# Destination bases of a sort read from a table instead of carried from step to step, and its record loads issued by SyncE

## The chip, the cores and the metric

The kernel runs on one core of a Trainium2 chip. The metric is the device time of one launch in microseconds (us); less is better. PE is the matrix engine, DVE the vector engine, ACT the scalar engine, POOL the GpSimd engine, SP the sync engine.

## The reference

Four graph layers on 6250 nodes with 128 features and 100000 edges, each added to its input:

```python
edge_index = jnp.stack([src, dst])          # src unsorted, dst sorted
for each of four layers:                    # attention, gated message, update, filter
    h = jnp.maximum(_layernorm(x), 0.0)
    x = x + layer(h, src, dst, edge attributes)   # gathers by one index, segment sums by the other
```

The first layer's attention needs for each edge a term of its destination, its softmax runs over the edges with one source (`segment_max` and `segment_sum` by `src`), and its sums run by `dst`. The later layers sum by either index. For this the kernel orders the edges by source before the layers run.

## The kernel before, in words

The edges are padded to 100352 = 784 tiles of 128 edges (`T`), the nodes are 49 blocks of 128 (`NB`). Eight tiles (`GT`) make a step, so a stage over all edges has 98 steps. The key of an edge is split into the number within its block (low part) and the block (high part).

The stages that the change touches run one after the other, with a barrier between them:

- `constants` makes the identity, triangular and all-ones matrices and loads keys and nodes.
- `front`, 98 steps: DVE makes one-hot rows of the low and high parts (L408, L409). PE sums them: `hs` counts the edges of each source (L466), and `hd` adds up over all steps, through an all-ones matrix, how many edges of each destination block stand in tile 0, 1, ... 7 of a step (L468). DVE reduces `hd` over the eight tiles to the 49 totals `tot_dst` (L416). The attention terms of the nodes are made beside it.
- `offsets`: from the counts, prefix sums give each source's first place (`start`) and each destination block's first place (`excl`, copied to `base_dst`, L585). 56 matmuls (L531) count slots meanwhile.
- `sort`, 98 steps: for each edge its place in the order by source (`rank`, into `idx`), its place in the order by destination (`drank`, kept in the record at `W_POS`) and its destination's attention term (`sj`, into the record at `W_SJ`) are worked out. POOL then writes each tile's 128 records of 512 bytes to `src_records` at those places, with one indirect DMA per tile (`send`, L798), 784 in all.

How `sort` is ordered: each engine runs its own loop, written by `run_steps` from a list of (stage, lag): in round r the stage works on step r - lag. The rounds of the engines are tied by semaphores alone:

- SP: `load_rows` (lag 0) loads the keys' low parts, spread over all partitions (two DMAs, L612), into one of two buffers.
- ACT: `load_records` (0), `wide_hot` (1), `low` (0), `keys` (2), `mask` (1), `carry` (2).
- PE: `prefix` (1), `same` (1), `late` (3), `rank` (2), `drank` (2), `early` (2).
- DVE: `bump` (2), `place` (3), `hot` (0), `finish` (3). The end of `finish` counts `placed` up (L676).
- POOL: `send` (0), which waits for `placed` and `keyed`.

The records lie in four buffers. `load_records` of step s waits until all eight sends of step s - 4 have landed (`sent`), and is the first thing in ACT's round. The destination bases are a running row: `drank` of a step starts from `dbase` (L759), adds the edges before it in its tile (L762) and the tiles before it (eight matmuls, L766), whose last 49 columns are the row for the next step. ACT copies them back to `dbase` in `carry` (L708), and `place` of step s doesn't take `drank` before that copy is done:

```python
wait_step(e, r["dranked"], st)
e.wait_ge(r["carried"], st.i + 2)
e.tensor_tensor(r["pick"][:, 0, :, :], ...)          # L657
```

Of the kernel before, what the change touches and what calls it, by code (L numbers as in the profile page):

```python
# [5 lines left out]
ALU = mybir.AluOpType  # L6
ACT = mybir.ActivationFunctionType
F32 = mybir.dt.float32
# [5 lines left out]
P = 128  # L14
# [4 lines left out]
GT = 8  # L19
# [198 lines left out]
def setup(kn, ctx):  # L218
# [22 lines left out]
    kn.base_dst = sb("base_dst", [P, NB])  # L241
# [10 lines left out]
    kn.tot_dst = sb("tot_dst", [P, NB])  # L252
# [19 lines left out]
def constants(kn):  # L272

    def sb(name, shape, dt):
# [5 lines left out]
        sb(n, [P, P], F16) for n in ("beforeh", "penh", "identh", "onesh", "iotah"))  # L280
    kn.kin = sb("kin", [P, 2, T], I32)
# [5 lines left out]
    def build(r):  # L287
# [7 lines left out]
        def vector(e, ch):  # L295
# [15 lines left out]
            ch(e.tensor_copy(kn.identh[:, :], kn.ident[:, :]))  # L311
            ch(e.tensor_copy(kn.onesh[:, :], kn.ones[:, :]))
# [46 lines left out]
def front(kn):  # L359
# [6 lines left out]
    def build(r):  # L366
        def vector(e, ch):
            e.memset(r["zero"][:, :], 0.0).then_inc(r["zero_ok"], 1)

# [46 lines left out]
            ch(e.tensor_reduce(kn.tot_dst[:, :], r["hd"][:, 0:GT * NB].rearrange("p (t b) -> p b t", b=NB), AX, ALU.add))  # L416
# [17 lines left out]
        def tensor(e, ch):  # L434
            for i in range(total):
# [27 lines left out]
                if i < n:  # L463
# [4 lines left out]
                    e.matmul(r["hd"][:, 0:GT * NB], kn.onesh[:, :], r["hi"][:, i % 2, 0, :, :].rearrange("p t b -> p (t b)"),  # L468
# [30 lines left out]
        def sync(e, ch):  # L499
            e.wait_ge(r["zero_ok"], 1)  # L500
            for c in range(7):
# [9 lines left out]
                 ("sij", [P, NB * 2 * HEADS], F32)],  # L511
# [4 lines left out]
def offsets(kn):  # L516
# [5 lines left out]
    def build(r):  # L522
        def tensor(e, ch):
            e.matmul(r["small"][:, 0:NB], kn.before[:, :], kn.count[:, 1, :], start=True, stop=True)
            e.matmul(r["small"][:, NB:2 * NB], kn.ones[:, :], kn.count[:, 1, :], start=True, stop=True,
                     skip_group_check=True).then_inc(r["sums"], 1)
# [11 lines left out]
        def vector(e, ch):  # L538
            ch(e.tensor_scalar(r["none"][:, :], kn.count[:, 1, :], 0.0, None, ALU.is_equal))
# [5 lines left out]
            ch(e.tensor_copy(r["tot"][:, 0:NB], kn.tot_dst[:, :]))  # L545
# [28 lines left out]
            for q in range(2):  # L574
                for c in range(nt):
                    ins = e.tensor_scalar(r["lt"][:, q, c, :], r["s"][:, :], r["val"][:, q, c:c + 1], None, ALU.is_gt)
                ins.then_inc(r["less"], 1)
            e.wait_ge(r["counted"], 2)
# [6 lines left out]
            ch(e.tensor_copy(kn.base_dst[:, :], r["excl"][:, 0:NB]))  # L585
            ch.wait()
            for q in range(2):
# [9 lines left out]
                      ("none", [P, NB], F32)],  # L597
               sems=["sums", "iota", "less", "counted"])


def sort(kn):
# [5 lines left out]
    def build(r):  # L607
        def sync(e, ch):
# [6 lines left out]

            e.wait_ge(kn.low_st, 32)
            run_steps(e, ch, [(load_rows, 0)], n)

        def vector(e, ch):
            e.memset(r["rec"][:, :, :, :], 0.0).then_inc(r["cleared"], 1)  # L620
            ch(e.memset(r["onerow"][:, :], 1.0))
# [27 lines left out]
            def place(st):  # L649
# [6 lines left out]
                e.wait_ge(r["carried"], st.i + 2)  # L656
# [22 lines left out]
        def scalar(e, ch):  # L679
            def load_records(st):  # L680
                wait_quad_free(e, r, "sent", st, GT)
                e.dma_start(r["rec"][:, st.quad, :, 0:NREC], rec_tiles[:, bass.ds(st.i * GT, GT), :]
                            ).then_inc(r[f"rec_ld{st.quad}"], 16)

# [21 lines left out]
            def carry(st):  # L706
                wait_step(e, r["dranked"], st)
                e.activation(r["dbase"][0:1, :], r["drank"][0:1, GT * NB:], ACT.Copy).then_inc(r["carried"], 1)  # L708

# [4 lines left out]
            e.wait_ge(r["cleared"], 1)  # L714
            e.activation(r["dbase"][0:1, :], kn.base_dst[0:1, :], ACT.Copy).then_inc(r["carried"], 1)
            run_steps(e, ch, [(load_records, 0), (wide_hot, 1), (low, 0), (keys, 2), (mask, 1), (carry, 2)], n, 4)
            ch.wait()

        def tensor(e, ch):
# [1696 lines left out]
```

## Time and profile before

| | |
|---|---|
| Median of three runs | 7450.98 us (7444.45 to 7451.76) |
| Profiled execution, own time | 7452.6 us |
| Its span, first to last instruction | 7451.0 us |
| Busy over the span | PE 65%, PE weight load 50%, DVE 63%, ACT 35%, POOL 60% |
| First to last send of `sort` | 332.4 to 1583.9 us |
| Mean granted clock of TensorE | 0.719 |

A span is read from the first instruction to the last; the own time of the profiled execution is 1.6 us longer. A line such as "ACT x L698 <- DMA y: 485.3, 50" says that ACT sat idle before its instruction of line 698 for 485.3 us in 50 cases, and that a DMA which writes y ended each of these. A share of busy time is a mean over some twenty stages with different limits; the change lies in the stages that end at 1596 us.

### The profile page before, as it was taken

Reading aid. Unit: us, or ns where it says so; the run is one execution under the profiler, and the core shown is the slowest. Engines: PE = TensorE matmul, PEld = TensorE weight load, DVE = VectorE, ACT = ScalarE, POOL = GpSimd, SP = SyncE. Lnnn points to the kernel's source line nnn. Section 1 sums busy time; section 2 is a strip of 40 time slices with the busy share of each in tenths; the row PEclk is TensorE's granted clock in tenths of the full one; section 3 lists DMA queues with packets and bytes.
Section 4 is the critical chain, followed back from the end, with each engine's and each line's share of the span. In section 5 each row is a group of like instructions: output and inputs, shape, how many; then the busy total and the mean of one; then the engine's idle time right before and its main releaser. Section 6 shows DMA issues by size and latency. Waiting matters only on the chain. (4 is left out here: it accounts for less than half of the span.)

```text
span 7451.0 us, 136629 instructions
## 1 busy us (share of the span) xinstructions
PE 4824.4 (65%) x26170; PEld 3695.7 (50%) x26171; DVE 4677.1 (63%) x15439; ACT 2640.5 (35%) x6893; POOL 4448.7 (60%) x5261
## 2 busy tenths in 40 slices
PE   6777777730555554773566666666667664998896
PEld 4555555520444443662355555334555554666664
DVE  8666665634444443666555555777777775777776
ACT  2244444410222222664400000563333334444443
POOL 0165666652777777662277777207777771777774
PEclk9978787765555555666566667788888886778777
DMA  1144444460222222441133333103333321333332
GB/s 59 51 119 118 120 119 119 117 71 20 58 58 58 58 57 71 113 112 48 43 78 78 78 78 78 25 15 78 74 74 74 75 68 31 73 72 72 72 72 52
DMA packets 858580, 541.08 MB, mean 73 GB/s; under 512 B 652181, under 2 KB 757481, under 8 KB 858089
## 3 DMA queue, kind: packets, MB, share of 16 engines
q0 software_dynamic: 148032, 300.00, 14.9%
q1 hardware_dynamic: 608520, 192.51, 12.5%
q10 hardware_dynamic: 101920, 47.37, 2.6%
q8 instruction: 40, 0.66, 0.0%
q14 instruction: 68, 0.55, 0.0%
HBM read 411.68 MB, written 127.68 MB: 72 GB/s over the span
## 5 line engine op out<-in xcount | busy, mean ns | idle before, releaser
L1339 POOL DMA_INDIRECT l2e_rows<-l_rows,l2e_idx x832 | 847.2, 1018 | 566.9 <-DVE l2e_idx L1347 328.4
L798 POOL DMA_INDIRECT src_records<-sort_rec,sort_idx x784 | 768.5, 980 | 552.4 <-DVEq L676 319.4
L1339 POOL DMA_INDIRECT l1e_rows<-l_rows,l1e_idx x832 | 796.8, 958 | 490.0 <-DVE l1e_idx L1347 296.3
L1339 POOL DMA_INDIRECT l3e_rows<-l_rows,l3e_idx x832 | 804.1, 967 | 424.8 <-DVE l3e_idx L1347 221.4
L1222 POOL DMA_INDIRECT dst_rows<-l0d_out,l0d_idx x832 | 812.3, 976 | 276.5 <-issue 196.7
L2115 PE MATMUL l2e_pV<-l2e_rows,ident 128*128 128x512 f32 x416 | 302.3, 817 | 355.6 <-DMA l2e_rows<-l_rows,l2e_idx 355.1
L1194 PE MATMUL l0d_pX<-table,l0d_ohT 128*128 x1664 | 461.2, 457 | 86.3 <-issue 69.3
L1321 PE MATMUL l0m_pR<-l0m_rows,l0m_oh 128*128 128x129 f32 x1664 | 352.8, 378 | 200.2 <-DVE h_nodes L1292 140.9
L1685 PE MATMUL l1e_pG<-k_weights,l1e_dT 64*128 64x128 f32 x1664 | 220.5, 403 | 374.7 <-DVE l1e_prod L1714 371.7
L1194 PEld LDWEIGHTS l0d_pX<-table,l0d_ohT 128*128 128x128 f32 x1664 | 393.1, 326 | 139.8 <-issue 139.7
L1186 PE MATMUL l0d_pT<-identb,l0d_oh 128*128 128x128 bf16 x832 | 125.4, 305 | 472.8 <-DVE l0d_oh L1167 472.8
L1321 PEld LDWEIGHTS l0m_pR<-l0m_rows,l0m_oh 128*128 128x128 f32 x1664 | 306.4, 276 | 246.7 <-issue 199.9
L1714 DVE TENSOR_TENSOR l1e_prod<-l1e_pG,l1e_rows 128x512 f32<-128x512 f32 x208 | 143.9, 692 | 447.9 <-DMA l1e_rows<-l_rows,l1e_idx 425.3
L1705 ACT ACTIVATE l1e_dT<-l1e_pD 128x256 f32<-128x256 f32 x208 | 79.9, 384 | 970.4 <-PE l1e_pD L1674 970.4
L2139 ACT ACTIVATE l2e_sq<-l2e_pV 128x128 f32<-128x128 f32 x832 | 219.1, 278 | 554.9 <-PE l2e_pV L2120 554.9
L1695 PE MATMUL l1e_pR<-l1e_oh,l1e_prod 128*128 128x128 f32 x1664 | 387.1, 405 | 6.3 <-DVE l1e_prod L1714 4.6
L1685 PEld LDWEIGHTS l1e_pG<-k_weights,l1e_dT 64*128 64x128 f32 x1664 | 169.6, 274 | 443.7 <-ACT l1e_dT L1705 174.7
L1130 DVE TENSOR_TENSOR l0d_t<-l0d_meta,l0d_dump 128x4 f32<-128x4 f32 x208 | 35.7, 172 | 555.9 <-DMA dst_rows<-l0d_out,l0d_idx 555.9
L2245 PE MATMUL l3e_pR<-l3e_oh,l3e_prod 128*128 128x128 f32 x1664 | 307.8, 342 | 103.9 <-issue 53.7
L2120 PEld LDWEIGHTS l2e_pV<-table,l2e_ohT 128*128 128x128 f32 x1664 | 296.5, 251 | 142.8 <-issue 142.8
L1695 PEld LDWEIGHTS l1e_pR<-l1e_oh,l1e_prod 128*128 128x128 f32 x1664 | 330.7, 295 | 47.2 <-issue 40.5
L2245 PEld LDWEIGHTS l3e_pR<-l3e_oh,l3e_prod 128*128 128x128 f32 x1664 | 259.9, 238 | 188.9 <-issue 188.3
(406 smaller groups left out, 13955.7 us busy)
## 6 DMA issues: line engine op xcount, KB each, us to landing
sort_rows<-lo_rows SPq DMA_DIRECT2D x196, 256.0 KB
sort_rec<-rec ACTq DMA_DIRECT2D x98, 472.0 KB
l0m_rows<-dst_rows SPq DMA_DIRECT2D x416, 66.0 KB, 2.0
l0m_rows<-dst_rows POOLq DMA_DIRECT2D x416, 66.0 KB
l1e_rec<-src_records SPq DMA_DIRECT2D x832, 32.0 KB
l2e_lrow<-dst_local SPq DMA_DIRECT2D x208, 128.0 KB
l3e_rec<-src_records SPq DMA_DIRECT2D x832, 25.0 KB
l0d_meta<-src_records SPq DMA_DIRECT2D x832, 6.0 KB
```

Source lines behind the costliest of these rows:

```text
L798: e.indirect_dma_start(kn.by_src_rec[:, :], bass.IndirectOffsetOnAxis(ap=r["idx"][:, st.quad, j:j + 1], axis=0), r["rec"][:, st.quad, j, : ...
L1194: ins = e.matmul(r["pX"][:, st.par, j, 0:TW], r["ohT"][:, st.quad, j, :], kn.tab0[:, bass.ds(blocks[j] * TW, TW)], start=True, stop=True)
L1222: e.indirect_dma_start(kn.by_dst[:, :], bass.IndirectOffsetOnAxis(ap=r["idx"][:, st.quad, j:j + 1], axis=0), r["out"][:, st.quad, j, :], N ...
L1321: ins = e.matmul(sums(r, st, j), r["oh"][:, st.par, j, :], r["rows"][:, st.ring, j, 0:AW], start=True, stop=True)
L1339: e.indirect_dma_start(r["rows"][:, st.quad, j, 0:width], None, table[:, :], bass.IndirectOffsetOnAxis(ap=r["idx"][:, st.quad, j:j + 1], a ...
L1685: ins = e.matmul(r["pG"][:, st.par, q, u * P:(u + 1) * P], r["dT"][at, st.par, u, :], w[at, :], start=True, stop=True)
L1695: ins = e.matmul(r["pR"][:, st.par, j, :], r["prod"][:, st.par, j, :], r["oh"][:, st.par, j, :], start=True, stop=True)
L1714: e.tensor_tensor(r["prod"][:, st.par, :, :].rearrange("p (u q) c -> p q u c", q=2), r["pG"][:, st.par, :, 0:2 * P].rearrange("p q (u c) - ...
L2115: e.matmul(r["pV"][:, st.quad, :, :].rearrange("p j c -> p (j c)"), kn.ident[:, :], r["rows"][:, st.quad, :, :].rearrange("p j c -> p (j c ...
L2120: ins = e.matmul(r["pV"][:, st.quad, j, :], r["ohT"][:, st.par, j, :], block(kn, kn.TB, blocks[j]), start=False, stop=(j == G - 1), skip_g ...
L2139: ch(e.activation(r["sq"][:, j, :], r["pV"][:, st.quad, j, :], ACT.Square, scale=H ** -0.5, accum_out=r["var"][:, st.par, j:j + 1]))
L2245: ins = e.matmul(r["pR"][:, st.par, j, :], r["prod"][:, st.par, j, :], r["oh"][:, st.par, j, :], start=True, stop=True)
```

## The change

The first stage keeps its sums by step. Its matmul for `hd` gets, instead of all ones, a matrix with ones in column i alone, so that row i of `hd` holds the 8 x 49 counts of step i (98 steps in 128 rows). `offsets` makes of it a table `tile_base` with the base of every (step, tile, block): group sums and two more matmuls, then, between the slots' comparisons and the wait for the 56 matmuls, seven additions that go from tile to tile, and a split into two half-precision parts (half the value, and what is left over). In `sort`, `drank` adds row i of that table to the edges before it in the tile by two matmuls, whose weights are column i of the identity (times 2, and times 1) spread over 128 columns. `carry`, `dbase` and the wait on `carried` go. `load_records` goes from ACT, where it had lag 0, to SP with lag 1, behind `load_rows`, with the same wait on `sent`; SP's loop is unrolled four steps instead of two and first waits for `cleared`, as ACT did before.

```diff
@@ constants @@
+            ch(e.tensor_scalar(kn.twiceh[:, :], kn.ident[:, :], 2.0, None, ALU.mult))
@@ front, vector @@
             e.memset(r["zero"][:, :], 0.0).then_inc(r["zero_ok"], 1)
+            ch(e.memset(r["to_row"][:, :], 0.0))
+            ch.wait()
+            ch(e.memset(r["to_row"][:, P:P + 1], 1.0))
+            ch.wait()
...
-            ch(e.tensor_reduce(kn.tot_dst[:, :], r["hd"][:, 0:GT * NB].rearrange("p (t b) -> p b t", b=NB), AX, ALU.add))
+            ch(e.tensor_copy(kn.tile_counts[:, :], r["hd"][:, 0:GT * NB]))
@@ front, tensor @@
-                    e.matmul(r["hd"][:, 0:GT * NB], kn.onesh[:, :], r["hi"][:, i % 2, 0, :, :].rearrange("p t b -> p (t b)"),
+                    e.matmul(r["hd"][:, 0:GT * NB], r["to_row"][:, P - i:2 * P - i], r["hi"][:, i % 2, 0, :, :].rearrange("p t b -> p (t b)"),
                              start=(i == 0), stop=(i == n - 1), skip_group_check=True).then_inc(r["pe"], 1)
@@ offsets, tensor @@
+            e.wait_ge(r["grouped"], 1)
+            e.matmul(r["small"][:, 2 * NB:3 * NB], kn.before[:, :], r["group"][:, :], start=True, stop=True,
+                     skip_group_check=True)
+            e.matmul(r["small"][:, 3 * NB:4 * NB], kn.ones[:, :], r["group"][:, :], start=True, stop=True,
                      skip_group_check=True).then_inc(r["sums"], 1)
@@ offsets, vector @@
+            counts = kn.tile_counts[:, :].rearrange("p (t b) -> p t b", b=NB)
+            e.tensor_reduce(r["group"][:, :], counts.rearrange("p t b -> p b t"), AX, ALU.add).then_inc(r["grouped"], 1)
...
-            ch(e.tensor_copy(r["tot"][:, 0:NB], kn.tot_dst[:, :]))
+            ch(e.tensor_copy(r["tot"][:, 0:NB], r["small"][:, 3 * NB:4 * NB]))
...
+            ch(e.tensor_tensor(r["row"][:, 0, :], r["small"][:, 2 * NB:3 * NB], r["excl"][:, 0:NB], ALU.add))
+            for t in range(GT - 1):
+                ch.wait()
+                ch(e.tensor_tensor(r["row"][:, t + 1, :], r["row"][:, t, :], counts[:, t, :], ALU.add))
+            ch.wait()
+            rows = r["row"][:, :, :].rearrange("p t b -> p (t b)")
+            ch(e.tensor_scalar(kn.tile_base[:, 0, :], rows, 0.5, None, ALU.mult))
+            ch.wait()
+            ch(e.scalar_tensor_tensor(kn.tile_base[:, 1, :], kn.tile_base[:, 0, :], -2.0, rows, ALU.mult, ALU.add))
             e.wait_ge(r["counted"], 2)
...
-            ch(e.tensor_copy(kn.base_dst[:, :], r["excl"][:, 0:NB]))
@@ sort, sync @@
+            def load_records(st):
+                wait_quad_free(e, r, "sent", st, GT)
+                e.dma_start(r["rec"][:, st.quad, :, 0:NREC], rec_tiles[:, bass.ds(st.i * GT, GT), :]
+                            ).then_inc(r[f"rec_ld{st.quad}"], 16)
             e.wait_ge(kn.low_st, 32)
-            run_steps(e, ch, [(load_rows, 0)], n)
+            e.wait_ge(r["cleared"], 1)
+            run_steps(e, ch, [(load_rows, 0), (load_records, 1)], n, 4)
@@ sort, vector @@
-            ch(e.memset(r["onerow"][:, :], 1.0))
...
-                e.wait_ge(r["carried"], st.i + 2)
@@ sort, scalar @@
-            def carry(st):
-                wait_step(e, r["dranked"], st)
-                e.activation(r["dbase"][0:1, :], r["drank"][0:1, GT * NB:], ACT.Copy).then_inc(r["carried"], 1)
-            e.wait_ge(r["cleared"], 1)
-            e.activation(r["dbase"][0:1, :], kn.base_dst[0:1, :], ACT.Copy).then_inc(r["carried"], 1)
-            run_steps(e, ch, [(load_records, 0), (wide_hot, 1), (low, 0), (keys, 2), (mask, 1), (carry, 2)], n, 4)
+            run_steps(e, ch, [(wide_hot, 1), (low, 0), (keys, 2), (mask, 1)], n, 4)
@@ sort, tensor @@
             def drank(st):
-                e.wait_ge(r["carried"], st.i + 1)
+                wait_step(e, r["hot"], st)
                 wait_step(e, r["dtaken"], st, 1)
-                e.matmul(r["drank"][:, 0:(GT + 1) * NB].rearrange("p (t b) -> p t b", b=NB), r["onerow"][0:1, :],
-                         r["dbase"][0:1, None, :].to_broadcast([1, GT + 1, NB]), start=True, stop=False,
-                         skip_group_check=True)
-                e.matmul(r["drank"][:, 0:GT * NB], kn.beforeh[:, :],
-                         r["ohhi"][:, st.quad, 0, :, :].rearrange("p t b -> p (t b)"), start=False, stop=False,
-                         skip_group_check=True)
-                for j in range(GT):
-                    ins = e.matmul(r["drank"][:, (j + 1) * NB:(GT + 1) * NB].rearrange("p (t b) -> p t b", b=NB),
-                                   kn.onesh[:, :], r["ohhi"][:, st.quad, 0, j:j + 1, :].to_broadcast([P, GT - j, NB]),
-                                   start=False, stop=(j == GT - 1), skip_group_check=True)
+                out = r["drank"][:, 0:GT * NB]
+                e.matmul(out, kn.beforeh[:, :], r["ohhi"][:, st.quad, 0, :, :].rearrange("p t b -> p (t b)"),
+                         start=True, stop=False, skip_group_check=True)
+                for k, t in enumerate((kn.twiceh, kn.identh)):
+                    ins = e.matmul(out, t[:, bass.ds(st.i, 1)].to_broadcast([P, P]), kn.tile_base[:, k, :],
+                                   start=False, stop=(k == 1), skip_group_check=True)
                 ins.then_inc(r["dranked"], 1)
```

## Rows read from the trace of the kernel before

**Rows 1.** Waits between 332 and 1585 us: waiter <- releaser, total us, times, longest.

```profile
...
ACT sort_ohTf L698 <- DMA src_records<-sort_rec,sort_idx: 485.3, 50, 13.0
DVE sort_pick L657 <- ACT sort_dbase L708: 374.9, 76, 9.4
...
POOL src_records L798 <- DVEq L676: 319.4, 55, 68.4
...
```

**Rows 2.** Tile sort_idx: duration in ns (min/median/max), first and last start in us.

```profile
...
L798 POOL DMA_INDIRECT src_records<-sort_rec,sort_idx x784: 956/962/1617, 332.4 to 1583.9; - x196
...
```

**Rows 3.** Groups of instructions, 0 to 2200 us: busy us, mean ns, idle before.

```profile
...
L798 POOL DMA_INDIRECT src_records<-sort_rec,sort_idx x784 | 768.5, 980 | 552.4 <-DVEq L676 319.4 <-issue 232.9
...
L766 PE MATMUL sort_drank<-sort_ohhi,onesh 128*128 128x392 f16 (+7 forms) x784 | 109.7, 291 | 0.0
...
L759 PE MATMUL sort_drank<-sort_dbase,sort_onerow 1*128 1x441 f32 x196 | 98.3, 579 | 0.0
...
```

**Rows 4.** Timeline of POOL, 1000 to 1110 us: start, us, instruction, idle before.

```profile
...
1029.51 0.96 POOL L798 DMA_INDIRECT src_records<-sort_rec,sort_idx  x1 [5.39 <-DVEq L676]
...
1048.66 0.96 POOL L798 DMA_INDIRECT src_records<-sort_rec,sort_idx  x1 [0.30 <-issue]
1054.87 0.96 POOL L798 DMA_INDIRECT src_records<-sort_rec,sort_idx  x1 [5.25 <-DVEq L676]
...
1059.93 1.26 POOL L798 DMA_INDIRECT src_records<-sort_rec,sort_idx  x1 [0.30 <-issue]
...
```

**Rows 5.** Timeline of all engines, 899 to 931 us.

```profile
...
902.49 0.57 DVE L644 TENSOR_TENSOR sort_prod<-sort_sj,sort_ohhi 128x392 f32<-128x392 f32 x1 [1.67 <-PE sort_sj L778]
...
909.60 0.96 POOL L798 DMA_INDIRECT src_records<-sort_rec,sort_idx  x1 [0.30 <-issue]
...
912.00 0.39 ACTq L682 DMA_DIRECT2D sort_rec<-rec  x1
...
912.48 1.06 ACT L698 ACTIVATE sort_ohTf<-sort_ohTs 128x1024 f32<-128x1024 f16 x1 [9.78 <-DMA src_records<-sort_rec,sort_idx]
...
918.03 0.19 ACT L708 ACTIVATE sort_dbase<-sort_drank 1x49 f32<-1x49 f32 x1
918.32 0.57 DVE L657 TENSOR_TENSOR sort_pick<-sort_drank,sort_ohhi 128x392 f32<-128x392 f32 x1 [6.86 <-ACT sort_dbase L708]
...
921.09 0.48 DVE L638 TENSOR_SCALAR sort_ohTs<-sort_rows,pcol 128x1024 f16<-128x1024 f16 x1
...
925.79 0.96 POOL L798 DMA_INDIRECT src_records<-sort_rec,sort_idx  x1 [5.11 <-DVEq L676]
...
```

**Rows 6.** Timeline of DVE, 315 to 346 us.

```profile
...
331.56 0.57 DVE L628 TENSOR_TENSOR sort_upto<-sort_prefix,sort_upto 128x392 f32<-128x392 f32 x1 [0.23 <-DVE sort_rec L674]
...
339.72 0.57 DVE L628 TENSOR_TENSOR sort_upto<-sort_prefix,sort_upto 128x392 f32<-128x392 f32 x1 [0.26 <-DVE sort_rec L674]
...
```

**Rows 7.** DMA queues, 906 to 911.1 us: packets, MB, share (q1 is SP's).

```profile
...
q1 hardware_dynamic: 288, 0.52, 35.7%
...
```

**Rows 8.** DMA queues, 912 to 915.6 us (q10 is ACT's).

```profile
...
q10 hardware_dynamic: 1040, 0.48, 57.0%
...
```

**Rows 9.** Timeline of all engines, 1058 to 1062 us.

```profile
...
1060.20 0.48 DVE L638 TENSOR_SCALAR sort_ohTs<-sort_rows,pcol 128x1024 f16<-128x1024 f16 x1
...
1060.60 0.48 DVE L639 TENSOR_SCALAR sort_ohTd<-sort_rows,pcol 128x1024 bf16<-128x1024 f16 x1
...
```

**Rows 10.** Timeline of all engines, 262 to 335 us.

```profile
...
296.46 0.58 DVE L582 CAST slot_reg<-offsets_tiles 32x416 int32<-32x416 f32 x1 [18.32 <-PE offsets_tiles L531]
...
304.51 25.01 SPq L612 DMA_DIRECT2D sort_rows<-lo_rows  x12
305.45 3.47 DVE L620 MEMSET sort_rec<- 128x4096 f32 x1 [1.86 <-PEq L215]
...
```

**Rows 11.** Tile front_hd, the reduction behind the first stage.

```profile
...
L416 DVE TENSOR_REDUCE tot_dst<-front_hd x1: 557/557/557, 259.1 to 259.1; 128x49 f32<-128x392 f32 x1
...
```

More of the change, by code:

```diff
@@ L240, in setup @@
     kn.local = sb("local", [P, 2, SLOTS])
-    kn.base_dst = sb("base_dst", [P, NB])
     kn.W = sb("k_weights", [P, len(MATS), H])
@@ L251, in setup @@
     kn.first_at = sb("first_at", [P, NB], I32)
-    kn.tot_dst = sb("tot_dst", [P, NB])
 def node_buffers(kn, ctx):
@@ L280, in constants @@
         sb(n, [P, P], F16) for n in ("beforeh", "penh", "identh", "onesh", "iotah"))
+    kn.twiceh = sb("twiceh", [P, P], F16)
+    kn.tile_counts = sb("tile_counts", [P, GT * NB], F32)
+    kn.tile_base = sb("tile_base", [P, 2, GT * NB], F16)
     kn.kin = sb("kin", [P, 2, T], I32)
@@ L510, in front @@
                  ("shift", [P, NB], F32), ("rest", [P, HEADS, NB], F32), ("sum", [P, 3], F32),
-                 ("sij", [P, NB * 2 * HEADS], F32)],
+                 ("sij", [P, NB * 2 * HEADS], F32), ("to_row", [P, 2 * P], F16)],
           sems=["zero_ok", "zeroed", "var_ok", "std", "scales", "hot", "pe", "normed", "turned", "hT_ok",
@@ L525, in tensor @@
             e.matmul(r["small"][:, NB:2 * NB], kn.ones[:, :], kn.count[:, 1, :], start=True, stop=True,
+                     skip_group_check=True)
+            e.wait_ge(r["grouped"], 1)
+            e.matmul(r["small"][:, 2 * NB:3 * NB], kn.before[:, :], r["group"][:, :], start=True, stop=True,
+                     skip_group_check=True)
+            e.matmul(r["small"][:, 3 * NB:4 * NB], kn.ones[:, :], r["group"][:, :], start=True, stop=True,
                      skip_group_check=True).then_inc(r["sums"], 1)
@@ L596, in offsets @@
                       ("lt", [P, 2, nt, SLOTS], F32), ("b", [P, 2, SLOTS], F32),
-                      ("none", [P, NB], F32)],
-               sems=["sums", "iota", "less", "counted"])
+                      ("none", [P, NB], F32), ("group", [P, NB], F32), ("row", [P, GT, NB], F32)],
+               sems=["grouped", "sums", "iota", "less", "counted"])
 def sort(kn):
@@ L679, in scalar @@
         def scalar(e, ch):
[L680 to L683, printed above, removed]
             def low(st):
@@ L805, in sort @@
     phase(kn, "sort", build, psums=[("same", [P, 2, 4, P], F32), ("prefix", [P, 2, BANK], F32),
-                                    ("rank", [P, BANK], F32), ("drank", [P, (GT + 1) * NB], F32),
+                                    ("rank", [P, BANK], F32), ("drank", [P, BANK], F32),
                                     ("sj", [P, 2, BANK], F32)],
@@ L810, in sort @@
                       ("ohTf", [P, 2, GT * P], F32), ("dist", [P, GT, P], F16), ("mask", [P, 2, GT, P], F16), ("pick", [P, 2, GT, NB], F32),
-                      ("prod", [P, GT, HEADS, NB], F32), ("idx", [P, 4, GT], I32), ("pos", [P, 2, GT], F32), ("upto", [P, 4, GT, NB], F32),
-                      ("dbase", [1, NB], F32), ("onerow", [1, P], F32)],
+                      ("prod", [P, GT, HEADS, NB], F32), ("idx", [P, 4, GT], I32), ("pos", [P, 2, GT], F32), ("upto", [P, 4, GT, NB], F32)],
                sems=["cleared", "bumped", "hot", "low", "widened", "turned", "prefixed", "same_done", "masked", "ranked", "dranked",
-                     "carried", "taken", "dtaken", "looked", "scored", "placed", "keyed"]
+                     "taken", "dtaken", "looked", "scored", "placed", "keyed"]
                     + [f"{m}{j}" for m in ("rec_ld", "sent") for j in range(4)],
```

## The prediction, made before the changed kernel ran

> **What bounds the kernel now.** The stages follow each other behind barriers, so the table of busy shares over the whole span says nothing here; I read the stages that the diff touches. The page's groups of instructions put the sends of `sort` first among the lines before 2200 us: 784 of them, 768.5 us busy, and they run from 332.4 to 1583.9 us [rows 2, 3]. With the last one's 0.96 us that is 1252.5 us, 12.8 us a step.
>
> I asked next what POOL does in that time. Its timeline has one pattern: sixteen sends (two steps) in a row, 0.96 us each with 0.30 us between, then a gap of a little over 5 us, which ends when DVE counts `placed` up [rows 4]. The table of waits sums these gaps: 319.4 us in 55 cases, of which 68.4 us is the one before the first send, so 251.0 us in 54 [rows 1]. The rest is POOL's own work: 768.5 us busy, and 232.9 us of gaps in which nothing is waited for [rows 3]. 768.5 + 232.9 + 251.0 = 1252.4 us; the sum closes.
>
> Then why POOL waits. The table of waits names two more: ACT waits 485.3 us in 50 cases, almost 10 us each and so in every second step, for sends to land, and DVE waits 374.9 us in 76 for ACT's `dbase` copy [rows 1]. The timeline of one cycle ties them together [rows 5]. The eighth send of a step starts at 909.60 and ends at 910.56. ACT, which stood at `load_records`, issues its load at 912.00, and only then does the rest of its round: `ohTf` from 912.48, the `dist` and mask work, and last the copy L708 at 918.03. DVE, idle for 6.86 us, takes `drank` at 918.32, works through `place`, `hot` and `finish`, and POOL goes on at 925.79. So from the end of the sends of step s to the start of those of step s + 2 it takes 925.79 - 910.56 = 15.2 us, while POOL has only step s + 1 to do, 8 x 1.26 = 10.1 us. The missing 5.1 us is the gap. It is a loop over two steps: 15.2 + 10.1 = 25.3 us, and two groups begin at 1029.51 and 1054.87 [rows 4], 25.36 us apart.
>
> **What the change does to this loop.** Two links go: ACT no longer stands still for `sent`, and DVE no longer waits for a copy at the end of ACT's round. Either edit alone would cut the chain from landed sends to `placed`. What sets the pace then?
>
> POOL's own work. 768.5 + 232.9, and 0.30 for each of the 54 removed waits (an ordinary gap stands there): 1017.6 us, or 10.4 us a step.
>
> A correction to it. A typical send takes 962 ns, the mean is 980 [rows 2, 3]: 784 x 18 ns = 14 us of slow sends. The one at 1059.93 took 1.26 us [rows 4] and ended at 1061.19, just behind the two `tensor_scalar` of `hot`, 1060.20 to 1061.08 [rows 9]. In the other step of a cycle `hot` (the row at 921.09, [rows 5]) falls into POOL's gap, so it meets a send in about one step of two. Without gaps it meets one in each: bounds are nothing more and 0.66 us for each of 98 steps (the slowest send, 1617 ns, less 962), 65 us in place of 14. I take 14 + 17 = 31 us, twice today's rate and a little over, since that rate is of this very pair. Sends: 1017.6 + 17 = 1035 us, 10.56 us a step.
>
> The Trainium skill bears on this ("SBUF — State Buffer", section "SBUF: two separate sides"): while DVE runs an operation in a mode that uses two ports, GpSimd can't write the descriptors of its DMAs and stands blocked to the end of that operation. The trace agrees with a send that ends 0.11 us behind the pair. Taken at its full, with each step's send held over both operations, it gives a time of its own, the rival "port" below.
>
> DVE. Left alone it needs 8.16 us a round: its `bump` of one step starts at 331.56 and of the next at 339.72 with no wait in between on another engine but its own order [rows 6], with the old `drank` behind it. That is 2.4 us under POOL's 10.56. PE gets shorter: two single-precision matmuls (579 ns each) and eight of L766 (291 ns) go, two of the 392-column kind come, with broadcast weights and a row index from a register, which the trace shows nowhere. Bounds: 0.29 us each as L766, 0.58 us each as L759 [rows 3]. Even at the upper end two in place of ten cost less than what goes, so I take nothing for them; the cover is the 2.4 us. The wait of `drank` on `hot` is of a step that `prefix` has waited for already. ACT loses its copy and its load's issue (0.39 us, [rows 5]).
>
> SP. This is where something is added: `load_records` of step s stands in SP's queue behind `load_rows` of s + 1, and behind it stands `load_rows` of s + 2. The rows of r + 1 now wait until the sends of r - 5 have landed, DVE's `hot` of that round waits for the rows, and `finish` of r - 2 stands behind `hot`. That is a new loop, over three steps: sends 10.1 us; last send to the issue 912.00 - 910.56 = 1.4; L, from the issue to the rows' landing; from `ohTs` to POOL's next start 925.79 - 921.09 = 4.7 [rows 5]. L: the queue of SP moved two row loads within the stretch 906 to 911.1 us, at most 5.1 us [rows 7], the queue of ACT a record load, issued at 912.00, by 915.6, 3.6 us, with all its 1040 packets [rows 5, 8]. One behind the other that is up to 8.7 us. The loop gives (10.1 + 1.4 + 8.7 + 4.7) / 3 = 8.3 us a step, under 10.56. It would set the pace only from L = 3 x 10.56 - 16.2 = 15.5 us on. Moving the load to SP costs nothing then.
>
> On that move the Trainium skill says ("DMA: Bandwidth & Descriptors", section "Issuing engines are not separate DMA queues") that DMAs started by any engine run on the same 16 DMA engines, so that another issuer saves only issue time, which by the row at 912.00 would be 0.39 us x 98 = 38 us of ACT's time. What the trace adds is that the issuer's wait moves too.
>
> **The other parts.** `front`: two memsets of 256 columns and two waits ahead of the first one-hot, about 0.4 us; the 98 matmuls keep their shape; a copy takes the place of a reduction of 0.56 us [rows 11]: 0. `offsets`: the reduction, 0.56 us, now precedes two more matmuls and the sums: +0.8 us. The ten new vector operations lie ahead of the wait for the 56 matmuls, where DVE stood idle for 18.32 us [rows 10]; at 0.3 us each with their waits they need 3 us of it. Were that cover gone, 3 us. `twiceh` lies under the loading of the keys. `sort`'s start: rows were loaded from 304.51 on, while DVE cleared `rec` until 305.45 + 3.47 = 308.92 [rows 10]; now they are issued after that, and land some 4 us later; bounds 0 and 4.4, I take 3.3, since part of it lies under `low` on ACT. Sum: +4.5 us. The drain behind the last send and all later stages stay.
>
> **The sum.** 1252.5 - 1035 = 217.5 us off, 4.5 on: -213. The profiled execution's own time is 7452.6 us, so 7239.6; the median of the runs lies 1.6 us lower: **7238 us**. This is faster by 2.9%; within 0.2% (15 us) a measurement of this kernel can't be told from no change.
>
> **Rivals.**
>
> - *Port* (0.06). Each step's send is held over both operations of `hot`, 0.88 us and the 0.11 behind them. 98 x 1.0 = 98 us in place of 14: 1018 - 14 + 98 = 1102 us of sends, 7305. The typical excess now (14 us over some 49 meetings, 0.3 us) speaks against it. By the Trainium skill's rule of the port lock it needs the send's descriptors to be written just when the pair starts.
> - *DVE and PE become the bound* (0.07). In the round from 902.49 on DVE waited 1.67 us for PE's `sj` [rows 5]. Twice that in each round (before the early and the late pair): 8.16 + 3.34 = 11.5 us a step, 1127 us, time 7330. Against it: PE loses work, and such waits followed PE's idle time.
> - *Slower* (0.05). The rows come late because they stand behind the records' wait in one queue, and all engines wait for them. It decides from L = 3 x 12.78 - 16.2 = 22.1 us on; at L = 24 us a step takes 13.4 us, 1313 us of sends, 7516. L is measured at up to 8.7 us with each load in a queue of its own, so a queue would have to take almost three times the sum.
> - *No change* (0.05). What ends POOL's gap is another chain over two steps that only ran beside the copy (`keyed`, or the records' landing before `place`), so that 25.3 us stay: 7455.
> - Quicker than 7213 (0.04): no send is held at all, 1018 - 14 = 1004 us, 7207.
>
> **Range and chances.** The likeliest case (0.73) runs from 1018 us of sends (7221) to 1069 (7272), and a few us on either side for the added parts. Taking in the port lock, 7213 to 7310 leaves out 0.07 + 0.05 + 0.05 and the lower end, about 2 in 10. Faster by over 0.2%: 0.91; slower: 0.05; the same: 0.04.
>
> **What would show it.** Right: POOL's gaps on `placed` sum to under 10 us behind the first, sends run from about 337 to 1371 us, no line waits long for sends on ACT or DVE but `hot` for rows, the group of slow sends grows to some 30 us (mean 1000 ns), and `drank` has three matmuls a step. Wrong: a wait of DVE for the rows' DMA that POOL's gap follows (the SP loop), DVE waits for `sj` in each round (PE), or gaps of 5 us that come back every two steps.

## The result, and the profile after

The changed kernel takes 7209.76 us (median of three runs, 7206.27 to 7227.38); the ratio to the kernel before is 0.9686, 95% interval 0.9672 to 0.97. The forecast was 7238 us, range 7213 to 7310: the direction and the main cause were right, and the median lies 3 us under the range. The profiled execution is the slowest of the three, 7227.38 us with a span of 7225.7 us, so it gained 225.2 us over the profiled one of before, where the forecast's sum said 213.

The runs of this document were made in seven groups. The kernels of one group ran on one chip, together with the kernel before. In two groups, of which this result is one, the kernel before took 7444 to 7451 us; in the five others it took 8871 to 9022 us. Below, "the first kind of chip" and "the second kind" stand for the two. Each experiment says which it was.

The whole gain of the profiled execution lies in one stretch. Tile `sort_idx` of the changed kernel, as in [rows 2]:

```profile
...
L808 POOL DMA_INDIRECT src_records<-sort_rec,sort_idx x784: 954/958/1765, 334.8 to 1358.7; - x196
...
```

The first send begins at 334.8 us (2.4 later than before), the last at 1358.7, so with the last one's 0.96 us the sends take 1024.9 us in place of 1252.5. These 227.6 us less and the later start of 2.4 make 225.2. What comes after the sends takes 7451.0 - 1583.9 = 5867.1 us before and 7225.7 - 1358.7 = 5867.0 us after: unchanged.

The group of sends (window 330 to 1590 us; busy, mean ns, idle before), against [rows 3]:

```profile
...
L808 POOL DMA_INDIRECT src_records<-sort_rec,sort_idx x784 | 786.2, 1003 | 308.8 <-issue 231.1 <-DVEq L701 77.7
...
```

Its idle time fell from 552.4 to 308.8 us, and the wait for `placed` from 319.4 to 77.7. The table of waits between 335 and 1360 us, against [rows 1]:

```profile
...
ACT sort_rec L728 <- DMA sort_rec<-rec: 322.8, 93, 9.4
...
PE sort_sj L788 <- DVE sort_prod L670: 246.3, 238, 3.1
POOL src_records L808 <- issue: 231.1, 758, 0.3
DVE sort_ohTs L664 <- DMA sort_rows<-lo_rows: 172.5, 90, 3.2
...
POOL src_records L808 <- DVEq L701: 77.7, 26, 70.1
...
```

70.1 of the 77.7 us are the wait before the first send; the other 25 cases hold 7.6 us, 0.30 each, an ordinary gap. Behind its first send POOL always finds the next one ready, as the forecast had it. ACT waits for records and DVE for rows in almost every step, and neither wait reaches POOL. The timeline of one step shows why:

```profile
...
519.26 0.97 DVE L357 TENSOR_TENSOR sort_ohhi<-khh,iotah 128x784 f16<-128x784 f16 x1
519.70 1.36 POOL L808 DMA_INDIRECT src_records<-sort_rec,sort_idx  x1 [0.30 <-issue]
...
521.77 0.49 DVE L664 TENSOR_SCALAR sort_ohTs<-sort_rows,pcol 128x1024 f16<-128x1024 f16 x1 [1.54 <-DMA sort_rows<-lo_rows]
...
525.93 0.57 DVE L654 TENSOR_TENSOR sort_upto<-sort_prefix,sort_upto 128x392 f32<-128x392 f32 x1 [0.26 <-DVE sort_rec L699]
...
526.35 0.38 SPq L639 DMA_DIRECT2D sort_rec<-rec  x1
...
527.01 0.88 SPq L633 DMA_DIRECT2D sort_rows<-lo_rows  x2
...
530.80 0.23 ACT L728 ACTIVATE sort_rec<-kin 128x16 f32 x1 [3.54 <-DMA sort_rec<-rec]
...
532.20 0.49 DVE L664 TENSOR_SCALAR sort_ohTs<-sort_rows,pcol 128x1024 f16<-128x1024 f16 x1 [1.98 <-DMA sort_rows<-lo_rows]
532.61 0.47 DVE L665 TENSOR_SCALAR sort_ohTd<-sort_rows,pcol 128x1024 bf16<-128x1024 f16 x1
532.77 1.14 POOL L808 DMA_INDIRECT src_records<-sort_rec,sort_idx  x1 [0.31 <-issue]
...
536.36 0.57 DVE L654 TENSOR_TENSOR sort_upto<-sort_prefix,sort_upto 128x392 f32<-128x392 f32 x1 [0.26 <-DVE sort_rec L699]
...
```

DVE's rounds follow each other at 525.93 and 536.36, 10.43 us apart, against 8.16 when left alone [rows 6]. 1.98 us of that it stands at `ohTs`, for the rows. SP issues the records at 526.35 and the rows from 527.01 on, and DVE has them at 532.20: L, the time from the issue of the records to the landing of the rows, is 5.9 us. The loop over three steps that the prediction built then comes to (10.1 + 1.4 + 5.9 + 4.7) / 3 = 7.4 us. It follows POOL's pace and doesn't make it.

### The profile page after: what moved, and what is told of

It reads as the page before. It is cut to its first block and busy times, and to the rows that moved or that the text cites. A ratio compares the mean times of both kernels' runs of the same rounds, so it can differ in the third digit from the quotient of the medians.

```text
span 7225.7 us, 135048 instructions
## 1 busy us (share of the span) xinstructions
PE 4663.0 (65%) x25390; PEld 3584.5 (50%) x25391; DVE 4674.3 (65%) x15451; ACT 2639.3 (37%) x6794; POOL 4459.9 (62%) x5261
## 5 line engine op out<-in xcount | busy, mean ns | idle before, releaser
L808 POOL DMA_INDIRECT src_records<-sort_rec,sort_idx x784 | 786.2, 1003 | 308.8 <-issue 231.1
L788 PE MATMUL sort_sj<-sj_parts,sort_ohTd 128*128 128x196 bf16 x2352 | 292.9, 277 | 247.0 <-DVE sort_prod L670 246.3
L788 PEld LDWEIGHTS sort_sj<-sj_parts,sort_ohTd 128*128 128x128 bf16 x2352 | 215.2, 108 | 325.6 <-DVE sort_prod L670 317.5
```

The source lines that it names most:

```text
L788: ins = e.matmul(r["sj"][:, u % 2, i * wide:(i + 1) * wide], t, kn.sjt[:, part, :, :].rearrange("p k b -> p (k b)"), start=(part == 0), st ...
L808: e.indirect_dma_start(kn.by_src_rec[:, :], bass.IndirectOffsetOnAxis(ap=r["idx"][:, st.quad, j:j + 1], axis=0), r["rec"][:, st.quad, j, : ...
```

## The experiments

### More PE work

```diff
-                e.matmul(out, kn.beforeh[:, :], ...  start=True, stop=False, ...)
+                for again in range(9):
+                    e.matmul(out, kn.beforeh[:, :], ...  start=True, stop=False, ...)
```

> The changed kernel with the first matmul of drank issued nine times in place of once (each starts the sum anew, so the result is the same): eight more matmuls of 392 columns in each step, as many as the old drank had. Where sends go out without gaps (kernel before near 7451): PE sat idle 246 us for DVE in the changed kernel's sort stage, so eight matmuls of 0.17 us each cost nothing: within 15 us of 7210. Where PE has gaps of its own (kernel before near 8870 or more): if PE sets the pace there, each step gets at least 8 x 0.17 = 1.3 us longer, 130 us over the kernel before; if sends do, nothing.

7213.36 us beside 7444.1 for the kernel before, ratio 0.9691 (0.9675 to 0.9707). The answer on tile `sort_drank` of this kernel, and PE's wait for DVE:

```profile
...
L775 PE MATMUL sort_drank<-sort_ohhi,beforeh x882: 326/329/535, 325.7 to 1315.5; 128*128 128x392 f16 x177
...
```

```profile
...
PE sort_sj L789 <- DVE sort_prod L670: 164.7, 205, 1.8
...
```

882 matmuls in place of 98, and the time is that of the changed kernel. Over the sends PE's busy time rises from 746 to 817 us, and its waits for DVE fall from 246.3 us to 164.7. The trace holds 7389 PE matmuls over the sends in the kernel before, 6605 in the changed kernel and 7387 here: the count is back where it was (all of the added ones in half precision, two of the old ones in single), and the gain stays. So the eight matmuls that the new `drank` saves a step in the trace are not where the gain comes from.

### More DVE work

```diff
+                for k in range(2):
+                    ch(e.tensor_copy(r["more"][:, k, :], r["drank"][:, 0:GT * NB]))
                 e.tensor_tensor(r["pick"][:, 0, :, :], r["drank"]...
```

> The changed kernel with two more DVE copies of 392 columns from PSUM in each step, about 0.5 us each. POOL theory (kernel before near 7451): DVE's round grows from 8.2 to 9.2 us, still under 10.4: within 15 us of 7210; if DVE were the bound, 98 us more. Where PE has gaps of its own: DVE waits for PE anyway, so less than half of the 98 us.

7220.16 us beside 7444.1, ratio 0.9696 (0.968 to 0.9712), so 10 us over the changed kernel's median and inside the 15 expected, where a bound on DVE would have given 98. Its two copies, and its wait for the rows:

```profile
...
L683 DVE COPY sort_more<-sort_drank x196: 555/557/558, 330.1 to 1328.3; 128x392 f32<-128x392 f32 x196
...
```

```profile
...
DVE sort_ohTs L664 <- DMA sort_rows<-lo_rows: 80.9, 84, 2.3
...
```

The copies take 196 x 0.557 = 109 us of instruction time (they overlap in part: DVE's busy time over the sends rises by 91 us), and DVE's wait for the rows shrinks from 172.5 to 80.9 us. DVE's slack is used up by about half and POOL notices nothing.

### A quarter of the record load

```diff
-                e.dma_start(r["rec"][:, st.quad, :, 0:NREC], rec_tiles[:, bass.ds(st.i * GT, GT), :]
+                e.dma_start(r["rec"][:, st.quad, 0:2, 0:NREC], rec_tiles[:, bass.ds(st.i * GT, 2), :]
```

> The changed kernel that loads the records of two of a step's eight tiles only (256 in place of 1024 packets, 0.12 in place of 0.48 MB a step); the other six tiles are sent with what their buffer holds, so the edge attributes in the output are not the reference's, while keys and places are. POOL theory (kernel before near 7451): the load is hidden, within 15 us of 7210. Where PE has gaps of its own: if DMA traffic in flight makes them, less traffic makes fewer: sends take 1438 us there with 310 us of such gaps, and the load is about a third of the stage's traffic, so some 100 us less than the kernel before; if they have another cause, nothing.

7219.96 us beside 7444.1, ratio 0.9703 (0.9687 to 0.9719): the size of the load in SP's queue doesn't matter to the time. DVE's wait for the rows behind it stays too, 173.2 us against 172.5. The kernels of these three experiments ran on one chip of the first kind; what the expectations say of a kernel before near 8870 us was not tried.

### The changed kernel again, and its parts taken back one by one

The kernel with the table but the loads on ACT, and the kernel with the loads on SP but the carried row:

```diff
 records_on_act, against the changed kernel
-            run_steps(e, ch, [(load_rows, 0), (load_records, 1)], n, 4)        # sync
+            run_steps(e, ch, [(load_rows, 0)], n)
-            run_steps(e, ch, [(wide_hot, 1), (low, 0), (keys, 2), (mask, 1)], n, 4)        # scalar
+            run_steps(e, ch, [(load_records, 0), (wide_hot, 1), (low, 0), (keys, 2), (mask, 1)], n, 4)
 carry_kept, against the kernel before
-            run_steps(e, ch, [(load_rows, 0)], n)
+            run_steps(e, ch, [(load_rows, 0), (load_records, 1)], n, 4)
-            run_steps(e, ch, [(load_records, 0), (wide_hot, 1), ..., (carry, 2)], n, 4)
+            run_steps(e, ch, [(wide_hot, 1), ..., (carry, 2)], n, 4)
 records_wait_3, against the changed kernel, in load_records
+                sent = (st.fourth + (st.quad == 3)) * (16 * GT)
+                if not isinstance(sent, int) or sent > 0:
+                    e.wait_ge(r[f"sent{(st.quad + 1) % 4}"], sent)
```

> The changed kernel once more, as the base of the others and to see whether its runs scatter. The theory (POOL's sends set the pace) expects sends of about 1025 us in the profile again (784 sends, 10.4 us a step, no wait but the first) and a time of 7205 to 7228 us. A theory by which chance in the first run made the gain expects a sends' stretch that differs by over 20 us.

> The changed kernel with the record loads back on ACT (lag 0); the table stays. POOL theory: DVE's place no longer hangs on ACT's round of the same step, but the mask work behind the load still does, over a chain of three steps (landed sends to issue 1.4, ACT's round 6, PE's round 8, place to placed 7.5, and 10.1 of sends: 33 us, 11.0 us a step against POOL's 10.4), so between all of the gain and three quarters of it: 7210 to 7275. Rival (ACT's stand at the load is the whole cause): the gaps stay, 7440 to 7455.

> The kernel before with one part of the change: the record loads go to SP (lag 1), the carried row and the wait on it stay. POOL theory: ACT stands no longer for landed sends, so the two-step loop is cut, DVE waits for the copy only as long as ACT's round lasts (6 us, under POOL's 10.4), and nearly the whole gain comes: 7205 to 7235. Rival (the wait on the copy is itself the limit): the gaps of 5 us in every second step stay, 7440 to 7455.

> The changed kernel in which the record load of step s waits also for the sends of step s - 3, so that the loop through SP's queue, the rows and DVE's hot closes over two steps in place of three. Loop as in the prediction with L as read in the changed kernel's trace (record load issued at 526.35, ohTs begins at 532.20, 5.9 us): (10.1 + 1.4 + 5.9 + 4.7) / 2 = 11.0 us a step, about 60 us over the changed kernel, 7265 to 7280; with L at the prediction's bound of 8.7 us 12.4 us a step, 7410. Rival (the rows are far ahead of their use, the queue's order doesn't matter): no change, 7205 to 7228.

`after_again` is the changed kernel without an edit. All four ran on a chip where the kernel before takes 8871.26 us. Ratios: the changed kernel 0.9997 (0.9979 to 1.0014), `records_on_act` 0.9986 (0.997 to 1.0001), `carry_kept` 1.002 (1.0004 to 1.0035), `records_wait_3` 0.9975 (0.9954 to 0.9996). The changed kernel, expected at 7205 to 7228 us, took 8862.12: a miss. It gains nothing there, so the other expectations, written for a kernel before of 7451 us, could not be judged. The trace of the changed kernel on that chip says what is different. First its sends, then its waits, then PE from 1000 us on:

```profile
...
L808 POOL DMA_INDIRECT src_records<-sort_rec,sort_idx x784: 952/958/1837, 334.3 to 1772.3; - x196
...
```

```profile
...
POOL src_records L808 <- DVEq L701: 502.7, 59, 69.8
...
PE sort_sj L788 <- issue: 121.5, 177, 9.3
PE sort_same L754 <- issue: 109.1, 109, 2.5
...
PE sort_prefix L740 <- issue: 99.6, 135, 2.5
...
```

```profile
...
1000.20 0.36 PE L740 MATMUL sort_prefix<-sort_ohhi,sort_ohlo 128*128 128x245 f16 x1 [1.11 <-issue]
1001.60 0.45 PE L740 MATMUL sort_prefix<-sort_ohhi,sort_ohlo 128*128 128x196 f16 x2 [1.03 <-issue]
1002.33 0.24 PE L740 MATMUL sort_prefix<-sort_ohhi,sort_ohlo 128*128 128x98 f16 x1 [0.28 <-issue]
1003.75 0.21 PE L740 MATMUL sort_prefix<-sort_ohhi,sort_ohlo 128*128 128x49 f16 x1 [1.18 <-issue]
1005.15 0.59 PE L750 MATMUL sort_same<-penh,identh 128*128 128x512 f16 x1 [1.20 <-issue]
...
```

The sends take 1438 us in place of 1024, with 502.7 us of waits for `placed`, and PE stands between its own matmuls, one or two of which come every 1.4 us, while the table names nothing that it waits for. In that stretch 268 such gaps are longer than 0.5 us, 310 us together; on the first chip the changed kernel has none. The label "issue" alone doesn't show that nothing was waited for: the trace of the kernel before, on the first chip, has it at 53 gaps of PE's first matmul of `prefix`, 316 us together, where the program does have a wait. But 147 of the 268 gaps, 176 us, lie between matmuls of `prefix` or of `same`, and within these stages the program has no wait. From 600 to 1200 us, 93% of the gaps begin less than 1.6 us after a send began, which holds for 70% of the time. They gather where sends are in flight; that the sends make them is not shown.

PE's busy time rises too, from 746 to 942 us, at a granted clock of 0.68 in place of 0.87. The first send starts at 334.3 us against 334.8: in the stages before, without sends, the two chips agree. Behind the last send 7091.4 us follow in place of 5867.0, so the later stages are longer as well, and what differs is not peculiar to the sort.

On this chip no part of the change makes a difference of over 0.4%. With the loads back on ACT the trace shows ACT waiting 373.9 us for landed sends again, and the sends take 1450 us against 1438.

`carry_kept` ran twice more, on two other chips:

> The kernel before with the record loads on SP and the carried row kept, once more, on a chip that may run the kernel before in 7451 us. As expected for the first run of it: nearly the whole gain, 7205 to 7235, ratio 0.968 to 0.972, if ACT's stand at the record load was the link that counted; 7440 to 7455 and gaps of 5 us in every second step if the wait on the copy was.

> The same kernel (record loads on SP, carried row kept) in search of a chip that runs the kernel before in 7451 us. Expected there: 7205 to 7235, ratio 0.968 to 0.972, if ACT's stand at the record load was the link that counted; 7440 to 7455 if the wait on the copy was.

8894.78 beside 8871.51 (1.0031, 1.0014 to 1.0048) and 8880.85 beside 8875.05 (1.0008, 0.9992 to 1.0024). Both chips were of the second kind, so the question stays open.

### More POOL work

```diff
+                ch.wait()
                 take_waits(e, kn.tally)
+                ch(e.iota(r["more"][:, :], [[1, SLOTS]], base=0, channel_multiplier=0))
                 for j in range(GT):
```

> The changed kernel with one more GpSimd instruction ahead of each step's eight sends: an iota of 832 columns into a buffer of its own, 0.82 us in the trace, which nobody reads. If POOL's instructions set the pace of the sort stage, each step gets the 0.82 us and some 0.1 of issue longer: 98 x 0.9 = 88 us over the changed kernel (7210 + 88 = 7298 where the kernel before takes 7451). If another engine or queue sets it and POOL has slack, it is within 10 us of the changed kernel. On a chip where the kernel before takes near 8870 us, PE's gaps set the pace by the first four profiles and nothing should be seen (under 20 us).

> The kernel before with the same iota ahead of each step's sends. By the loop of the prediction (15.2 us from the end of one step's sends to the start of those two steps on, and the sends themselves once) two steps get longer by one iota, not two, since the other one's lies in POOL's gap of 5 us: 49 x 0.9 = 44 us, 7495. If POOL's instructions had set the pace before the change too, 88 us, 7539. If the loop did not run through the sends, 0.

A chip with 9022.32 us for the kernel before: 8932.86 us, ratio 0.9896 (0.9767 to 1.0024, two runs of the kernel), and 9033.91 us, 1.0 (0.9968 to 1.0032). The first ratio is too wide to tell 20 us, and the changed kernel without the iota did not run on this chip. Its trace does show that POOL has slack there: beside the 98 iotas it still waits 301.5 us for DVE. For the second kernel the expected 44 us was for a kernel before of 7451 us. A longer POOL cost it nothing beyond the interval (0.32% is 29 us), so on this chip neither POOL's work nor the loop through the sends set its pace. Of the first kind of chip that says nothing.

### More PE work on the second kind of chip

```diff
 against carry_kept, in drank
+                for again in range(8):
+                    e.matmul(r["drank"][:, 0:GT * NB], kn.beforeh[:, :], ...  start=True, stop=False, ...)
                 e.matmul(r["drank"][:, 0:(GT + 1) * NB]...  r["onerow"][0:1, :], r["dbase"]...
```

> The kernel with the record loads on SP and the carried row kept, and eight more matmuls of 392 columns in each step's drank (overwritten by the sum that follows, so the result is the same). Where the kernel before takes 7451 us: 7205 to 7240 if the loads' move alone cuts the loop (PE has slack, by the run drank_more); 7440 or more if the wait on the copy is the limit. Where it takes near 8870 us and PE has gaps of its own: this kernel without the eight matmuls took 8888 and 8895 us; if PE's own work and instructions set the pace there, 8 x 0.17 x 98 = 130 us more, near 9020; if not, 8870 to 8900.

9147.9 us beside 8984.98, ratio 1.0173 (1.0133 to 1.0213), against 1.0008 to 1.0031 without the eight matmuls: 1.4 to 1.6% more, 130 to 150 us. The busy time of each engine over the sends (columns: us, then PE, PE weight load, DVE, ACT, POOL busy, granted clock as a share of full speed, DMA share, GB/s), first the first run of `carry_kept`, then this kernel:

```profile
...
337.90:1802.00 1464.10, 1095.33 (x7405) 787.08 (x7402) 776.38 (x1347) 554.24 (x1324) 772.18 (x784) 0.71 0.33 99
...
```

```profile
...
337.50:1965.90 1628.40, 1241.13 (x8173) 894.27 (x8170) 778.18 (x1347) 557.06 (x1324) 759.89 (x783) 0.77 0.30 89
...
```

The added matmuls in the trace of this kernel:

```profile
...
L761 PE MATMUL sort_drank<-sort_ohhi,beforeh x784: 326/534/534, 324.4 to 1943.8; 128*128 128x392 f16 x196
...
```

The extra time came out near the 130 us expected, but not for the reason expected. The expectation took 0.17 us for a matmul. Here their median length is 534 ns, against 329 ns for the same matmul in `drank_more` (granted clock over the sends 0.77 against 0.94). Eight in a row take 2.79 us at that length, and over the sends they keep PE busy for 258 us. Only about half of that reaches the kernel's time. So the second kind of chip feels added PE work, where the first kind doesn't, but PE's length alone doesn't set the pace there. In the two traces, which are of two chips, PE's busy time rises by 146 us and the stretch by 164. PE's gaps over 0.5 us with nothing named get fewer (142, 168 us together, against 239, 236 us), and its waits for DVE grow from 35 to 183 us. On the chip of `carry_kept_pe` the kernel before is itself 114 us slower, so the ratios are the safer comparison. What the changed kernel does with more PE work on such a chip was not tried.

## Why the prediction was right, point by point

- **Where the time was.** The loop over two steps and its gap of 5.1 us are gone. Right, and shown by the two traces: 251.0 us of waits behind the first before, 7.6 after. Of these 243.4 us, 17.7 went into longer sends (786.2 us busy against 768.5) and the ordinary gaps lost 1.8, which leaves the 227.5 that the sends gained.
- **POOL's own work sets the new pace.** Well supported for the first kind of chip: POOL has no gap over 0.31 us between its sends, and eight more matmuls, two more copies or a quarter of the record load leave the time (0.9691, 0.9696 and 0.9703 against 0.9686). That a longer POOL would lengthen the kernel there was not tried; the run for it fell on the second kind.
- **The size: 1035 us of sends, measured 1024.9.** The busy time is right, 785.5 forecast and 786.2 measured. Off is the term of the ordinary gaps. I carried over the 232.9 us of gaps without a wait and added 0.30 for each wait that went, 249 us in all; measured are 231.1 + 7.6 = 238.7. In the trace before, seven gaps of 1.86 us or so stand among them, each a few sends behind a wait; after the change the longest is 0.3. They went with the waits, 7 x 1.56 = 11 us. One of them, in POOL's timeline of the kernel before from 512 to 518 us:

```profile
...
512.70 0.96 POOL L798 DMA_INDIRECT src_records<-sort_rec,sort_idx  x1 [5.12 <-DVEq L676]
515.52 0.96 POOL L798 DMA_INDIRECT src_records<-sort_rec,sort_idx  x1 [1.87 <-issue]
...
```

- **Slow sends.** 31 us forecast; in the trace after, the sends over 1.0 us, 108 of them, lie 34.9 us above 0.96 each. The number came out right, but not by the prediction's reading. It took the send at 1059.93 to be held by the two `tensor_scalar`. That send began while the `tensor_tensor` of `both_hot` ran, which the prediction left out, and before the pair began. From the trace before:

```profile
...
1059.32 0.97 DVE L355 TENSOR_TENSOR sort_ohhi<-khh,iotah 128x784 f16<-128x784 f16 x1
...
```

  The same from the trace after, at its clearest:

```profile
...
643.70 0.97 DVE L357 TENSOR_TENSOR sort_ohhi<-khh,iotah 128x784 f16<-128x784 f16 x1
643.73 1.76 POOL L808 DMA_INDIRECT src_records<-sort_rec,sort_idx  x1 [0.30 <-issue]
...
```

  All sends sorted by where they begin show a pattern: a send that begins while `both_hot` runs is longer by what is left of it, less about 0.13 us. In the trace after it is 0.79 us longer with 0.92 left, 0.39 with 0.52 left, and not longer with 0.11 left. A send that had begun before is not lengthened at all. For the pair this holds less evenly: 43 sends that begin 0.1 to 0.2 us into one of the two are 0.19 us longer with 0.32 left, 15 that begin earlier in it hardly at all.

  In the trace before, 43 sends begin in a `both_hot` (14.7 us longer in sum) and 4 in one of the pair (0.7 us); in the trace after 74 (25.2 us) and 71 (8.7 us). So of the growth 10.5 us come from `both_hot`, at nothing in the prediction, and 8.0 from the pair, put at 17: two errors that cancel, which is luck.

  The Trainium skill's port rule ("SBUF — State Buffer", section "SBUF: two separate sides") counts in a DVE operation with two SBUF inputs when the GpSimd operation reads SBUF, and `both_hot` has two; this trace agrees with that. The rival "port", which has a send of each step held over the whole pair, is refuted: 35 us, not 98.
- **DVE.** 8.16 us of its own round held nearly: the step shown above takes 10.43 us, of which 1.98 are the wait for rows, and its busy time over the sends is 770 us in both traces. It waits 172.5 us for rows, which a further 1 us of copies a step cut to 80.9.
- **PE.** The two broadcast matmuls take 327 ns each, between the bounds of 0.29 and 0.58 and nearer the first; hidden, as costed.
- **SP's queue.** L was put at up to 8.7 us and is 5.9. The loop over three steps stays under POOL's pace. Whether it binds when it closes over two steps (`records_wait_3`) could not be judged.
- **The added parts.** 4.5 us forecast, 2.4 measured at the first send. The rows:

```profile
...
297.54 0.58 DVE L604 CAST slot_reg<-offsets_tiles 32x416 int32<-32x416 f32 x1 [14.99 <-PE offsets_tiles L542]
...
306.44 3.47 DVE L647 MEMSET sort_rec<- 128x4096 f32 x1 [1.87 <-PEq L215]
...
310.00 1.76 SPq L633 DMA_DIRECT2D sort_rows<-lo_rows  x4
...
314.19 0.48 DVE L664 TENSOR_SCALAR sort_ohTs<-sort_rows,pcol 128x1024 f16<-128x1024 f16 x1 [3.36 <-DMA sort_rows<-lo_rows]
...
```

  `front` and `offsets` cost 1.1 us (297.54 against 296.46 in [rows 10]), the 1.2 forecast; the ten vector operations took 18.32 - 14.99 = 3.3 us of DVE's idle time, 3 forecast. The start of `sort` was put at 3.3 us: DVE does wait 3.36 us for the first rows, but only 1.3 of them reach the first send.
- **"Either edit alone would cut the chain".** Open. The runs that split the change, `records_on_act` once and `carry_kept` three times, all fell on the second kind of chip, where the whole change gains nothing. Whether the table, the move of the loads or only both together give the gain is not known.
- **From the profiled execution to the median.** I took 1.6 us off, since the runs before lay within 8 us. The changed kernel's runs scatter over 21 us, and the median lies 17.6 under the profiled one; this, with the 12 us above, puts it 3 us under the range. How far sends can differ shows in `drank_more`, another kernel on another chip, profiled at 7213.43 us: its sends take 991 ns on average for 1003, 9.6 us less in sum:

```profile
...
L809 POOL DMA_INDIRECT src_records<-sort_rec,sort_idx x784 | 776.6, 991 | 310.4 <-issue 232.3 <-DVEq L701 78.0
...
```

  There 66 sends begin in a `both_hot` and are 15.9 us longer in sum, against 74 and 25.2 us. That the three runs of the changed kernel differ by the same is likely but not shown, since only one of them has a trace.
- **The rivals.** No change and slower: refuted on the first kind of chip. DVE and PE as the bound: refuted there. On the second kind the whole forecast fails: the change gains nothing, and PE has gaps that the first trace didn't show at all. A forecast from one trace holds for the chips that behave like it. The stated chances don't quite add up either: by the rivals' list "faster" has 0.90 and "the same" 0.05, not 0.91 and 0.04.

## What to carry to other kernels

When an engine's gaps come back every second step, look for the wait that stands at the head of another engine's round: what is queued behind it can close a loop over several steps. Such a loop can be cut by moving the wait to another queue, or by taking away what hangs on the work behind it. Here both were done at once, and their shares are not known. Work out the new loop that the move closes, with its number of steps, and look for the next engine's own length and its slack; here a count of sends times their pitch gave the new length of the sends to 1%. When you put a slow instruction down to another engine's work, look at what ran when it began, not at what ran when it ended. And run the kernel on more than one chip: here the whole gain of 3.1% was absent on the chips of the second kind.

## What the runs showed of the hardware that was not expected

- In five of seven groups of runs the same kernel before took 8871 to 9022 us in place of 7444 to 7451. In the changed kernel's trace from such a chip PE has 268 gaps of over 0.5 us within 1438 us of sends, 1.16 us on average, in front of one or two matmuls, with nothing named that it waits for. They gather where sends are in flight (93% of their beginnings against 70% of the time). What makes them, and what differs between the groups, stays open. One chip was used in two groups and was slow in both, the others in one each, so that it is the chip and not its condition at the time is not shown either.
- POOL's seven gaps of 1.86 us vanished together with its waits, without a change in its own instructions. What makes them is not shown.
- An indirect DMA on POOL that begins while DVE runs `both_hot` (0.97 us) lasts longer by the rest of that operation less about 0.13 us, up to 0.80 us; one that had begun first takes its usual 0.96 us.
- The granted clock of PE over the sends differs between the traces. Before, after, the changed kernel on the second kind of chip:

```profile
...
332.40:1583.90 1251.50, 901.43 (x7389) 706.34 (x7386) 769.99 (x1347) 539.03 (x1323) 767.56 (x783) 0.80 0.41 116
...
```

```profile
...
334.80:1358.70 1023.90, 746.13 (x6605) 597.07 (x6603) 770.47 (x1347) 538.01 (x1221) 785.21 (x784) 0.87 0.48 142
...
```

```profile
...
334.30:1772.30 1438.00, 941.78 (x6605) 702.51 (x6603) 773.25 (x1347) 532.90 (x1221) 763.41 (x783) 0.68 0.34 101
...
```

  0.80, 0.87 and 0.68 of full speed, with PE busy 72%, 73% and 65% of the stretch. `drank_more`, busier (81%), was granted 0.94, but `dve_more_psum`, with PE busy 77%, only 0.82: the busy share alone doesn't order them. The changed kernel's clock also differs between the two kinds of chip, 0.87 and 0.68. That lengthens PE's matmuls and not the gaps, during which none runs.
